# A fused attention and mixture-of-experts kernel: the PSUM bank of the turnings becomes the fifth bank of the working ring

## The reference

```
x = x + LN(attention(LN(x)))
x = x + LN(ffn(LN(x)))

attention: 16 heads of 16 features; 8 blocks of 64 tokens per batch; a block of
  queries sees all keys (first and last block) or its neighbours and the first and
  last block (the others); softmax over the seen keys, then the weighted values
ffn: xn = layernorm(x); a = gelu(xn @ abel_w + b)
  logits = xn @ gate; the best 2 of 8 experts, softmax of their two logits
  expert e: gelu(xn @ ew1[e] + eb1[e]) @ ew2[e] + eb2[e]
  m = (weighted sum of the two experts) @ expm(gens[0]) @ expm(gens[1]) @ expm(gens[2])
  g = sigmoid([a, m] @ gc_w + gc_b);   out = x + a*(1-g) + m*g
```

## Time and profile before

| | |
|---|---|
| median of 3 runs | 1752.6 us (1749.86 to 1754.69) |
| profiled execution, its own time | 1753.1 us |
| its span, first to last instruction | 1751.3 us |
| mean granted TensorE clock | 0.965 |
| PE busy | 1516.0 us, 87% |
| DVE busy | 1223.2 us, 70% |
| ACT busy | 896.1 us, 51% |
| POOL busy | 696.6 us, 40% |
| `front`'s steps 3 to 14 | 60.6 us each |

### The profile page before, as it was taken

How to read it: one execution, slowest core, us unless ns; L and a number is a source line. 1 busy time by engine, 2 the same in 40 slices (tenths; PEclk the granted TensorE clock), 3 DMA queues, 4 the chain that set the end, 5 groups by cost and what they waited for, 6 DMA issues and landing times. The chain is left out here.

```text
span 1751.3 us, 33300 instructions
## 1 busy us (share of the span) xinstructions
PE 1516.0 (87%) x10277; PEld 1049.1 (60%) x10342; DVE 1223.2 (70%) x3687; ACT 896.1 (51%) x1782; POOL 696.6 (40%) x705
## 2 busy tenths in 40 slices
PE   7889889989988998999899898799999999999500
PEld 5655455545545554555455466688888888888400
DVE  5667787888788787878877846356555656565287
ACT  3146766776676667667666664233333333333244
POOL 1011233533442443245334325144444444444468
PEclk9999999999999999999999999899999999999855
DMA  8132244345435533543554338656565665655397
GB/s 230 42 109 81 87 151 152 118 134 171 134 105 168 164 113 120 176 140 105 161 161 119 104 131 262 159 104 139 113 137 120 132 121 129 124 123 98 47 330 236
DMA packets 186076, 243.04 MB, mean 139 GB/s; under 512 B 23576, under 2 KB 156576, under 8 KB 185824
## 3 DMA queue, kind: packets, MB, share of 16 engines
q1 hardware_dynamic: 159360, 205.40, 37.3%
q0 software_dynamic: 26592, 36.07, 12.4%
HBM read 133.12 MB, written 105.64 MB: 136 GB/s over the span
## 5 line engine op out<-in xcount | busy, mean ns | idle before, releaser
L1112 ACT ACTIVATE pexp<-scT 128x512 f32<-128x512 f32 x768 | 433.4, 598 | 254.3 <-PE scT L868 222.6
L1317 DVE TENSOR_REDUCE mx<-work 128x1 f32<-128x320 f32 (+2 forms) x1024 | 500.3, 546 | 62.2 <-PE work L841 61.5
L1882 POOL DMA_INDIRECT y_rows<-rows_add,row_of x142 | 225.5, 1588 | 292.0 <-DMA y_rows<-rows_add,row_of 229.7
L841 PE MATMUL work<-w 126*128 126x320 bf16 (+4 forms) x1280 | 269.3, 295 | 30.4 <-DVE mx L1317 27.3
L868 PE MATMUL scT<-w 128*128 128x192 bf16 (+3 forms) x1472 | 261.5, 270 | 35.1 <-ACT pexp L1112 30.6
L1914 PE MATMUL h_ps<-inT,w1c 128*128 128x256 f32 x1136 | 259.5, 382 | 2.4 <-DVE inT L1966 2.4
L1927 PE MATMUL o_ps<-w,hT 128*128 x1136 | 256.8, 379 | 0.0
L1857 ACT ACTIVATE rows_add<-rows_out,row_share 128x257 f32<-128x257 f32 x142 | 64.6, 503 | 350.5 <-DVE rows_out L1982 301.3
L1914 PEld LDWEIGHTS h_ps<-inT,w1c 128*128 128x128 f32 x1136 | 217.3, 192 | 33.1 <-issue 3.3
L868 PEld LDWEIGHTS scT<-w 128*128 128x128 bf16 x1536 | 123.3, 97 | 173.5 <-ACT pexp L1112 126.9
L1927 PEld LDWEIGHTS o_ps<-w,hT 128*128 128x128 f32 x1136 | 210.5, 190 | 25.8
(11 more groups left out here) (204 smaller groups left out, 2065.6 us busy)
## 6 DMA issues: line engine op xcount, KB each, us to landing
w<-split_spill SPq DMA_DIRECT2D x384, 128.0 KB, 2.9
split_spill<-split SPq DMA_DIRECT2D x64, 384.0 KB, 3.1
rows_in<-z_rows SPq DMA_DIRECT2D x71, 265.0 KB, 4.8
y_rows<-pre SPq DMA_DIRECT2D x16, 514.0 KB, 5.6
y<-y_rows SPq DMA_DIRECT2D x16, 514.0 KB, 6.8
x_rows<-x SPq DMA_DIRECT2D x16, 512.0 KB, 2.8
abel_rows<-pre SPq DMA_DIRECT2D x16, 512.0 KB, 3.7
abel_in<-abel_rows SPq DMA_DIRECT2D x16, 512.0 KB, 4.6
```

The lines of the kernel that those rows point to most:

```text
L841: ins = nc.tensor.matmul(out[:, at:at + hi - lo], tile(qst[par][0:K_SCORE, h, :], t), kst[par][0:K_SCORE, h, lo:hi], start=True, stop=True)
L1112: nc.scalar.activation(pexp[:, (q * GROUP + n) % NPB, :], scT[n % 2][:, :], ACT.Exp, scale=DH ** -0.5).then_inc(s_exp, 1)
L1317: emptied(nc.vector.reduce_max(mx[:, c:c + 1], bank(s, "max", b, h, t)[:, 0:n], AX_X), s, "max", b, h, t)
L1882: pool.indirect_dma_start(kept.y_rows, bass.IndirectOffsetOnAxis(ap=row_of[n][:, r:r + 1], axis=0), rows_add[n % 2][:, r, :], None, comput ...
```

## The change

The bank `turn` becomes `work[4]`; the ring has five banks, and item i uses bank i modulo 5. The turnings of x (`xt`), of the context (`ctx`, all batches and not only the last) and of the maxima (`turnmax`) become items of the ring, at the place in the order where TensorE issues them, so the semaphores `s_xt`, `s_xnT`, `s_mt`, `s_m2`, `s_turn` and `s_ctxn` go. On ScalarE, `evac_xnT` moves from behind the four exponentials of quads 8 and 10 to behind the first of them, and `first_max(s-1, 1)` from behind the four of quad 3 to behind the third. On VectorE `second_max(s-1, 1)` moves from behind the six maxima of quad 3 to behind the fourth (where the step projects a batch).

```
-        work = [ps(f"work{i}", [P, S]) for i in range(4)]
+        work = [ps(f"work{i}", [P, S]) for i in range(5)]
-        turn = ps("turn", [P, S])
...
@@ def order_of(s):
+            if s < 0:
+                return [("xt", k) for k in range(KC)]
...
                 if here(s, 0):
                     seq.append(("project", m))
+                if here(s, 2) and m % 2:
+                    seq.append(("ctx", m // 2))
...
             for q in range(QUADS):
+                if q in TURN_XN and s + 1 < B:
+                    seq.append(("xt", TURN_XN.index(q)))
                 for n in range(GROUP):
                     if here(s, 0) and q < V_QUADS and n == 1:
                         seq.append(("value", q))
+                    if here(s, 2) and q < 2 and n == 2:
+                        seq.append(("ctx", q + 2))
+                    if here(s, 1) and q == LATE_TURN_AT and n == 2:
+                        seq.append(("turnmax", 1))
                     if here(s, 0):
                         maxima(s, fill(q, n))
                         if q == QUADS - 1:
+                            if n == 3:
+                                seq.append(("turnmax", 0))
                             maxima(s, late("end", n))
...
-            AT[s_, what_] = len(AT) % 4, len(AT) // 4
+            AT[s_, what_] = len(AT) % 5, len(AT) // 5
...
@@ def turn_max(b, part):
                 reduced(pe, b, part)
-                if part:
-                    pe.wait_ge(s_m2[0], b + 1)
-                    wait(pe, s_ctxn, b * NTOK)
-                else:
-                    wait(pe, s_ctxn, (b - 1) * NTOK)
-                    pe.wait_ge(s_xnT, min(b + 2, B) * KC)
+                out = use(b + part, "turnmax", part)
...
@@ def evac_ctx(b, g):   (ScalarE)
-                if g == 0:
-                    wait(act, s_turn, b * NTOK)
+                if g == 0 and b > 0:
+                    for j in range(NTOK):
+                        full(act, b + 1, "ctx", j)
...
@@ ScalarE, step
                     for n in range(GROUP):
                         if attend:
                             exps(s - 1, q, n)
+                        if q in TURN_XN and n == 0 and s + 1 < B:
+                            evac_xnT(s + 1, TURN_XN.index(q))
+                        if attend and q == LATE_TURN_AT and n == 2:
+                            first_max(s - 1, 1)
...
-                    if attend and q == LATE_TURN_AT:
-                        first_max(s - 1, 1)
...
-                    if q in TURN_XN and (not isinstance(s, int) or s + 1 < B):
-                        evac_xnT(s + 1, TURN_XN.index(q))
...
@@ VectorE, finish_a(b, j)
-                    ins.then_inc(s_ctxn, 1)
-                    dve.wait_ge(s_ctxn, b * NTOK + j + 1)
+                emptied(ins, b + 2, "ctx", j)
+                freed(dve, b + 2, "ctx", j)
...
@@ VectorE, step
                         for n in range(1, GROUP):
+                            if n == 3 and attend and q == LATE_TURN_AT:
+                                second_max(s - 1, 1)
                             for h, t in fill(q, n):
                                 maximum(s, s, h, t)
...
-                    if attend and q == LATE_TURN_AT:
+                    if attend and not proj and q == LATE_TURN_AT:
                         second_max(s - 1, 1)
```

More of the change, by code:

```diff
@@ L371, in front @@
         s_xn = sem("s_xn")
[L372 to L375, removed]
+        w_full = [sem(f"w_full{i}") for i in range(5)]
+        w_free = [sem(f"w_free{i}") for i in range(5)]
         s_part1 = sem("s_part1")
@@ L380, in front @@
         s_stack = [sem(f"s_stack{i}") for i in range(2)]
-        s_mt = [sem(f"s_mt{i}") for i in range(2)]
         s_m1 = [sem(f"s_m1{i}") for i in range(2)]
-        s_m2 = [sem(f"s_m2{i}") for i in range(2)]
         s_mrow = [sem(f"s_mrow{i}") for i in range(2)]
@@ L388, in front @@
         s_ctxT = sem("s_ctxT")
-        s_turn = sem("s_turn")
         s_rden = sem("s_rden")
-        s_ctxn = sem("s_ctxn")
         s_cbn = sem("s_cbn")
@@ L532, in front @@
         AT = {}
-        for s_, what_ in [(s_, what_) for s_ in range(B + 1) for what_ in order_of(s_)] + order_behind():
+        for s_, what_ in [(s_, what_) for s_ in range(-1, B + 1) for what_ in order_of(s_)] + order_behind():
             if what_[0] == "late z":
                 s_, what_ = B + 1, ("z",) + what_[1:]
-            AT[s_, what_] = len(AT) % 4, len(AT) // 4
+            AT[s_, what_] = len(AT) % 5, len(AT) // 5
         def bank(s, *what):
@@ L629, in put_maxima @@
             def put_maxima(par, b, part):
-                sp.wait_ge(s_m2[part], b + 1)
+                freed(sp, b + part, "turnmax", part)
                 heads = slice(EARLY, HEADS) if part else slice(0, EARLY)
@@ L793, in turn_xn @@
             def turn_xn(b, k):
[L796 to L799, removed]
+                out = use(b - 1, "xt", k)
                 for j in range(NTOK):
                     pe.wait_ge(s_xn, b * NTOK + j + 1)
-                    ins = nc.tensor.transpose(turn[:, j * P:(j + 1) * P], xn[:, j, k * P:(k + 1) * P],
+                    ins = nc.tensor.transpose(out[:, j * P:(j + 1) * P], xn[:, j, k * P:(k + 1) * P],
                                               ident_sb[:, :])
-                ins.then_inc(s_xt, 1)
+                filled(ins, b - 1, "xt", k)
             def project(b, m):
                 if m == 0:
-                    pe.wait_ge(s_xnT, (b + 1) * KC)
+                    for k in range(KC):
+                        freed(pe, b - 1, "xt", k)
                     if b == 0:
@@ L849, in turn_max @@
                 reduced(pe, b, part)
-                if part:
-                    pe.wait_ge(s_m2[0], b + 1)
-                    wait(pe, s_ctxn, b * NTOK)
-                else:
-                    wait(pe, s_ctxn, (b - 1) * NTOK)
-                    pe.wait_ge(s_xnT, min(b + 2, B) * KC)
+                out = use(b + part, "turnmax", part)
                 plain(pe)
                 some = mx[:, NT * EARLY:] if part else mx[:, 0:NT * EARLY]
-                nc.tensor.transpose(turn[0:some.shape[1], 0:P], some, ident_sb[:, :]).then_inc(s_mt[part], 1)
+                filled(nc.tensor.transpose(out[0:some.shape[1], 0:P], some, ident_sb[:, :]),
+                       b + part, "turnmax", part)
             def score_unit(b, par, q, n):
@@ L893, in turn_ctx @@
                     pe.wait_ge(s_ctxT, (b + 1) * NG)
[L894 to L902, removed]
+                out = use(b + 2, "ctx", j)
                 for g in range(NG):
@@ L905, in turn_ctx @@
                                               ident_sb[:, :])
[L906 to L909, removed]
+                filled(ins, b + 2, "ctx", j)
             def turn_z(s, b, zp, k):
@@ L1070, in evac_xnT @@
             def evac_xnT(b, k):
-                act.wait_ge(s_xt, b * KC + k + 1)
-                nc.scalar.copy(xnT[:, k, :], turn[:, :]).then_inc(s_xnT, 1)
+                full(act, b - 1, "xt", k)
+                emptied(nc.scalar.copy(xnT[:, k, :], bank(b - 1, "xt", k)[:, :]), b - 1, "xt", k)
             def first_part(b, m):
@@ L1086, in first_max @@
             def first_max(b, part):
-                act.wait_ge(s_mt[part], b + 1)
+                full(act, b + part, "turnmax", part)
                 wait(act, s_mrow[part], b * N_MAX * 16)
-                nc.scalar.copy(mrow[part][:, 0, :], turn[0:mrow[part].shape[0], 0:P]).then_inc(s_m1[part], 1)
+                nc.scalar.copy(mrow[part][:, 0, :], bank(b + part, "turnmax", part)[0:mrow[part].shape[0], 0:P])\
+                  .then_inc(s_m1[part], 1)
             def norm_x(b, p, j):
@@ L1321, in second_max @@
                 dve.wait_ge(s_m1[part], b + 1)
-                nc.vector.tensor_tensor(mrow[part][:, 1, :], turn[0:mrow[part].shape[0], 0:P],
-                                        mrow[part][:, 0, :], ALU.subtract).then_inc(s_m2[part], 1)
+                emptied(nc.vector.tensor_tensor(mrow[part][:, 1, :],
+                                                bank(b + part, "turnmax", part)[0:mrow[part].shape[0], 0:P],
+                                                mrow[part][:, 0, :], ALU.subtract), b + part, "turnmax", part)
             def evac_z(s, b, k):
@@ L1333, in finish_a @@
             def finish_a(b, j):
[L1335 to L1340, removed]
+                full(dve, b + 2, "ctx", j)
+                src = bank(b + 2, "ctx", j)
                 tv = src[:, :].rearrange("p (h e) -> p h e", e=32)
```

## The result

| | before | after |
|---|---|---|
| median beside each other | 1751.71 us (4 runs) | 1736.56 us (4 runs, 1734.54 to 1737.19) |
| profiled execution, its own time | 1753.1 | 1736.45 |
| span | 1751.3 | 1734.6 |
| a steady step (start of project 0 to the next) | 60.61 | 59.93 |
| first matmul of the experts | 1115.4 | 1099.4 |

The ratio is 0.9913, 95% interval 0.9898 to 0.9928. The forecast was 1741 (1735 to 1751), faster. Further on, L815 is L818, L885 L884, L916 (the turning of z) L904, L1301 L1291 and L1348 L1335.

The account below looks back on a forecast made before the run. TensorE sets the pace, so only its waits can shorten a step. 10.9 + 0.6 + 1.0 + 3.4 + 1.0 - 5.2 = 11.7 us off 1753.1 gives 1741.4; forecast 1741 us, range 1735 to 1751.

Parts of the forecast that it names:

- Dense 1, 13 x 0.84: Quad 1, steps 3 to 15: dense 1 no longer waits for a maximum; 0.84 us a step, 10.9 us gained.
- the first rival: Quad 3: the gain at dense 1 comes back as a wait at fill 5; 1752.3 us, chance 0.17.
- The late turning, 0.35 lost: Steps 1 to 15: quad 4's first maximum waits for `second_max`; 0.35 us a step, 5.2 us lost.
- the same distance holds: Quad 3, steps 1 and 2, without routing: the late turning costs the same 0.35 us a step there.
- Quad 9, 0.05: Quad 9: fill 6 starts earlier, but x's turning then waits; 0.05 us a step, 0.6 us in 13 steps.
- part 2: Quad 3 to 4, late turning of the maxima: 0.35 us a step lost, with 0.05 us from release to start.
- the 1.0 for that step: Step 15: with no turning of x, the 0.6 us gain stays whole in two places, less a give-back; 1.0 us.
- Step 0's squarings, 3.4: Step 0's four periods: the first squaring product waits for an earlier reduction; 0.86 us a period, 3.4 us gained.
- Step 16, 1.0: Step 16: the third turning's 0.58 us wait goes and dense 1 gains as in other steps; 1.0 us in sum.
- Behind the loop, 0: Tail of `front` and the experts: they keep their order, so no change, 0 us.
- the turnings cost nothing: Quad 4: the late turning's delay is absorbed by later waits for exponentials; 1736 us, chance 0.08.
- whole-ring rival: From 100 us to the end of `front`: all 34.3 us of ring waits go; 1718.8 us, chance 0.02.

Follow-up runs that it names:

- e7: Kernel before, four banks, with the first of quad 1's three maxima reduced ahead of context 3 on VectorE: 1737.91 us, ratio 0.9931.
- e4: Changed kernel with `second_max` behind the second maximum of quad 3 instead of the fourth: 1731.91 us, ratio 0.9884.
- e10: e9 with ScalarE's normalising of the context between the exponentials of quad 4 instead of quad 5: 1710.27 us, ratio 0.9768.
- e1: Kernel before, separate bank kept, with only the three moves on ScalarE and VectorE: 1749.37 us, ratio 0.9996.
- e9: e8 with VectorE's routing also cut in two pieces: 1726.23 us, ratio 0.9793.
- e2: Changed kernel with its ring counted modulo four, the turnings still in the ring and the fifth bank idle: 1798.29 us, ratio 1.0196.
- e8: e4 with VectorE's second statistics in three pieces: 1728.02 us, ratio 0.9800.
- e5: Changed kernel with `evac_xnT` back behind the fourth exponential of quads 8 and 10: 1769.72 us, ratio 1.0038.
- e6: Changed kernel with the second turning of x at the head of quad 11 instead of quad 10: 1729.27 us, ratio 0.9874.
- e3: Changed kernel with `second_max` back behind the sixth maximum of quad 3: 1752.82 us, ratio 1.0013.
- e11: e10 with the second turning of x at quad 11 instead of quad 10: 1712.04 us, ratio 0.9774.
- second group: e2, e5, e8 and e9, run beside the kernel before, which took 1763.6 us there (13 runs).
- first and third groups: First: e1, e3, e4 and e7, beside the kernel before at 1750.1 us; third: runs beside the kernel before at 1751.9 us.

## Why the prediction was right

The mechanism and the sign held; the sum was 11.7 and the chip gave 15.2 between the medians, 16.65 between the profiled executions. A part of the 16.65 is chance (items 4 and 5). By its steps:

**1.** *Dense 1, 13 x 0.84.* Right: 0.85 in each step, nothing returned in quad 3 (the 0.62 and 0.29 there moved along), and `e7` gets it in another way. Had it been given back, as the first rival had it, the step would not have got shorter.
**2.** *The late turning, 0.35 lost.* Right in steps 3 to 15, and `e4` gives it back. Wrong in steps 1 and 2: "the same distance holds" did not. Without a routing VectorE is further ahead, its fourth reduction and `second_max` are over before TensorE asks, and no wait is there: 13 times, not 15, 0.7 us off the sum.
**3.** *Quad 9, 0.05.* Mis-sized. The prediction put the turning of x "some 0.2 behind" the reduction that frees its bank, ending at 505.33. It starts 0.06 behind the end: 496.74 against 495.60 + 0.40 + 0.68 = 496.68. 505.39 would have been right on the old scale, a gain of 0.23, less 0.06 for slower matmuls behind a wait: 0.17, in 13 steps 2.2 us instead of 0.6. The 0.05 from release to start, which part 2 used, should have been used here too. In step 15, where no turning follows, one instead of two waits is still 1.04 long:
```profile
974.91 0.39 PE L844 MATMUL work<-w 126*128 126x512 bf16 x1 [1.04 <-DVE mx L1307]
```

That is against the 0.29 of the earlier trace rows and a 0.89 ahead of it, as in the earlier trace rows; and the other place, waits of 0.10 and 0.29 before, has none left; so of the 1.0 for that step about a half came.

**4.** *Step 0's squarings, 3.4.* Right: 4 x 0.84 = 3.4, and nothing more behind them. The other 1.1 of step 0 came ahead of them and is chance: the first 16 projections took 9.07 us and 10.15 before, but 8.5 to 10.1 in the ten traces with the turnings in the ring (10.09 in `e10`), and 9.41 in `e1` with the old bank. Missed were the turnings of batch 0. The two had one bank between them and the second waited 0.68 for ScalarE's copy; now they are one row:
```profile
9.99 2.71 PE L804 MATMUL work<-ident_sb,xn 128*128 128x128 f32 x8 [9.99 <-ACT xn L1085]
13.43 2.04 PE L818 MATMUL work<-xnT,wqkv 128*128 128x512 f32 x2 [0.72 <-issue]
```

Before, the second started at 12.29 and the projection at 14.09. The prediction looked at the ring's items and forgot that the turnings themselves, all in one bank before, had waits of their own.
**5.** *Step 16, 1.0.* Too small: 2.35. The same omission: contexts that had one bank now have five. From the first context to the first score behind the squarings' turnings it takes 994.15 - 986.40 = 7.75 us, before 1010.40 - 1000.96 = 9.44: 1.7, of which 0.58 is the wait that was predicted. A part is the clock: granted were 0.78 after and 0.70 before. Other traces part the two: `e4`, with the ring of five, takes 8.40 at 0.65, and `e1`, with the old bank, 8.98 at 0.81, where its second context waits 0.43 for VectorE. So 1.0 to 1.2 of the 1.7 is the ring.
**6.** *Behind the loop, 0.* Wrong, and of the other sign. 16.9 us were gained by the end of the loop, 14.1 by the end of the last dense items, in the trace after:
```profile
1060.97 2.21 PE L904 MATMUL work<-ident_sb,z 128*128 128x128 f32 x8 [2.62 <-DVE z L1541]
1064.09 6.09 PE L915 MATMUL work<-wab,zT 128*128 128x265 f32 x16 [0.92 <-DVE zT L1321]
```

and before:
```profile
1077.94 1.64 PE L916 MATMUL work<-ident_sb,z 128*128 128x128 f32 x8 [1.65 <-DVE z L1556]
1080.50 3.82 PE L927 MATMUL work<-wab,zT 128*128 128x265 f32 x16 [0.92 <-DVE zT L1330]
```

The same 16 matmuls take 6.09 instead of 3.82 us; 1.9 us of it were made up before the experts start.

The rival "the turnings cost nothing" named 1736, almost the measured time, for a wrong reason: they cost 2.3 us a step before the bank, and 0.35 at quad 4 with it. The time came out 4.4 us under the forecast, by items 2 to 5 less item 6, none of them over 1.7 us. Of these, 1.1 us in item 4 and some 0.6 in item 5 belong to the two traces and not to the change, about as much as the traces are further apart than the medians. The whole-ring rival was out by 18 us. `e9` shows what it would have taken: VectorE's long absences cut, not more banks; and then, by `e10`, ScalarE's order limits.

As for the rule of the Trainium skill on repeating gaps (Perfetto Trace Analysis, Optimization Strategy), which the prediction weighed: the gap in quad 3 (0.6 in step 7, 0.4 in the others) stayed with one more bank, and left when VectorE's routing was cut in two.

## What to carry to other kernels

Before adding a bank to an in-order ring, write down for each item which one it waits for, before and after; whatever joins the ring with the bank uses it up, and what had been serialised in the old side bank gains as well. How long an item holds its bank counts as much as the number of banks: a quarter-microsecond operation placed four reductions later undid what a step had gained (60.91 us, 60.61 before the change). Where the waits repeat at the places where the releasing engine is away (a routing, statistics), cut that stretch into pieces or move one release ahead of it first: `e7` gave the change's gain with no bank at all. Look at what the moved piece now stands ahead of, which in `e9` gave most of the gain back. After two such cuts the next engine's order is the one to look at.

## What was not expected of the hardware

TensorE's clock fell at one more place in the changed kernel, by the rows of two stretches, first after, then before (columns as in rows 1):
```profile
1062.00:1068.00 6.00, 5.08 (x14) 3.87 (x15) 1.77 (x5) 0.78 (x1) 3.35 (x4) 0.50 1.00 268
```
```profile
1079.00:1085.00 6.00, 5.08 (x25) 4.24 (x25) 3.27 (x11) 0.78 (x1) 3.33 (x4) 1.00 0.89 281
```
0.50 is the level of 1.2 GHz, 1.00 that of 2.4. Both show 5.08 us busy, for 14 matmuls or 25: the busy time alone does not tell. Ahead of it TensorE stood still for 2.62 us, before for 1.65, and then did eight small turnings and waited 0.92 more in both. The same 16 matmuls took 3.82 in `e1`, `e7`, `e2`, `e8`, `e9` and `e5` (idle 1.65, 1.65, 1.20, 1.15, 0.99 and 0.92 before the turnings), and 5.43, 6.78, 6.69, 5.80 and 5.50 in `e4`, `e6`, `e3`, `e10` and `e11` (idle 2.62, 2.62, 2.62, 1.93 and 1.93). So of all thirteen traces the seven with the shorter idle times took 3.82 us, and the six in which TensorE stood still longer for VectorE's `z` took 1.6 to 3 us more for what came next. A run that fills this idle time with other matmuls, to show the link, was not made.

In all four traces of the second group ScalarE stands still 5.1 to 5.2 us before one pair of exponentials in step 16, with nothing in the profile that releases it but an outside event. In `e9`:
```profile
1032.08 1.09 ACT L1101 ACTIVATE pexp<-scT 128x512 f32<-128x512 f32 x2 [5.20 <-remote]
```
Neither the trace after nor those of the first and third groups have it there. In the trace after the idle time at that place is 0.46. If the kernel before had it in that group, too, which no trace shows, it would be 4 to 5 of the 12 us by which its runs are longer there; what it is stays open, and no step length above includes it.
